# Feed-forward of odd chunks begun in the next batch's context attentions

## The reference, cut to what matters

```python
x = L0(x, ctx, ctx, fside, fside)      # 16 heads of 64 over 64 context rows, bias added twice, residual, LayerNorm
h1 = ln(x);  x = attn(h1, h1, ...) + x        # 16 heads of 32 over the 1024 rows; q, k, v and weights rounded to 8 bits
h2 = ln(x);  x = attn(h2, context, ...) + x   # the same over the 64 context rows
h3 = ln(x)
a, g = split(h3 @ ff_w1 + ff_b1)              # 512 -> 2 x 2048
x = a * gelu(g) @ ff_w2 + ff_b2 + x           # 2048 -> 512
```

## Time and profile before

| what | us |
|---|---|
| median of 3 runs | 3792.23 (3792.03 to 3795.36) |
| the profiled execution, its own time | 3793.03 |
| its span, first to last instruction | 3791.2 |
| context attention of chunk 2, chunk 3 | 116.4, 118.2 |
| self-attention and middle of chunk 2 | 164.0, 134.9 |
| self-attention and middle of chunk 3 | 168.2, 146.6 |
| context attention of chunk 4, chunk 5 | 114.8, 120.0 |
| self-attention and middle of chunk 4 | 162.5, 134.5 |
| context attention of chunk 6, chunk 7 | 115.1, 120.6 |
| self-attention and middle of chunk 6 | 164.1, 135.1 |

### The profile page before, as it was taken

The page is one execution under the profiler, slowest core; times in us unless marked ns, Lnnn a source line. Parts: engine busy times, 40 slices in busy tenths (PEclk is TensorE's granted clock), DMA queues, the critical chain, the costliest instruction groups (busy, mean ns, idle before and its releaser), DMA issues.

```text
span 3791.2 us, 50839 instructions
## 1 busy us (share of the span) xinstructions
PE 3003.7 (79%) x19712; PEld 2180.3 (58%) x19712; DVE 2182.8 (58%) x3575; ACT 1621.5 (43%) x2666; POOL 1328.7 (35%) x1025
## 2 busy tenths in 40 slices
PE   4446646779967799989967798989977798989999
PEld 4335433445756565755756565755756565755677
DVE  2334539778445568468455577468455577468431
ACT  3412126557422267357422267257322167257321
POOL 1132327445232234245231244245241244244221
PEclk8678765689988899989988899999988899999999
DMA  6883644312343332422343332432443322422334
GB/s 209 293 297 119 236 150 153 149 61 79 134 151 141 137 117 79 149 102 79 144 146 139 133 117 79 150 112 79 157 140 145 126 105 75 150 111 79 144 122 178
DMA packets 232046, 518.20 MB, mean 137 GB/s; under 512 B 96768, under 2 KB 117504, under 8 KB 209792
## 3 DMA queue, kind: packets, MB, share of 16 engines
q1 hardware_dynamic: 219392, 513.33, 37.2%
q10 hardware_dynamic: 12416, 1.62, 0.3%
HBM read 428.39 MB, written 82.31 MB: 135 GB/s over the span
## 4 chain that ended last, share of the span: by engine, by line
PE 58%; DVE 18%; issue 7%; ACT 6%; POOL 6%; DMA 4%; SPq 2%; ACTq 1%; POOLq 0%; DVEq 0%
PE psum L1494 16%; PE psum L1495 15%; PE psum L1496 15%; PE psum L1770 5%; DVE mx L1374 4%; PE psum L1760 3%; DVE w1T L1393 2%; PE psum L1784 2%; DVE stats L1263 1%; DVE den L1380 1%; DMA kept<-st_lo 1%; ACT e L1080 1%; DVE x L1259 1%; POOL rstd L767 1%; SPq L502 1%
## 5 line engine op out<-in xcount | busy, mean ns | idle before, releaser
L809 POOL TENSOR_SCALAR w1b<-e,rec 128x1024 f16<-128x1024 f32 x512 | 572.7, 1119 | 810.4 <-DVE rec L1382 699.3
L1374 DVE TENSOR_REDUCE mx<-psum 128x1 f32<-128x1024 f32 x512 | 624.6, 1221 | 216.9 <-PE psum L1761 214.4
L1080 ACT ACTIVATE e<-psum,nb,scale 128x1024 f32<-128x1024 f32 x512 | 616.7, 1205 | 16.7
L1494 PE MATMUL psum<-h_hi,fw_hi 128*128 128x512 f32 x1024 | 452.7, 442 | 2.2 <-DVE h_lo L1170 2.2
L1770 PE MATMUL psum<-ident,w1b 128*128 128x128 f16 x4096 | 348.1, 234 | 126.2 <-DVE w1T L1393 115.1
L1770 PEld LDWEIGHTS psum<-ident,w1b 128*128 128x128 f16 x4096 | 259.4, 104 | 270.2 <-issue 227.2
L1495 PE MATMUL psum<-h_lo,fw_hi 128*128 128x512 f32 x1024 | 411.2, 402 | 0.0
L1496 PE MATMUL psum<-h_hi,fw_lo 128*128 128x512 f32 x1024 | 411.0, 401 | 0.0
L1393 DVE TENSOR_SCALAR w1T<-psum 128x1024 bf16<-128x1024 f16 x512 | 347.1, 678 | 42.6 <-PE psum L1770 40.4
L1494 PE MATMUL psum<-w_hi,ht_hi 128*128 128x512 f32 x640 | 269.0, 420 | 71.0 <-DVE e L1317 37.2
L1259 DVE TENSOR_TENSOR x<-psum,x 128x512 f32<-128x512 f32 x224 | 152.7, 684 | 271.2 <-PE psum L1496 271.2
(11 more groups left out here) (170 smaller groups left out, 6070.8 us busy)
## 6 DMA issues: line engine op xcount, KB each, us to landing
fw_hi<-pieces SPq DMA_DIRECT2D x192, 512.0 KB, 3.2
fw_lo<-pieces SPq DMA_DIRECT2D x192, 512.0 KB, 4.2
w_hi<-kept SPq DMA_DIRECT2D x80, 1024.0 KB, 4.9
w_lo<-kept SPq DMA_DIRECT2D x80, 1024.0 KB, 7.6
fbias<-in_fside_Bx16xSxS SPq DMA_DIRECT2D x64, 256.0 KB, 3.8
prep_raw<-in_L_xattn_ff_w SPq DMA_DIRECT2D x12, 1024.0 KB, 8.0
pieces<-prep_hi SPq DMA_DIRECT2D x24, 512.0 KB, 3.5
pieces<-prep_lo SPq DMA_DIRECT2D x24, 512.0 KB, 5.5
```

What stands on the lines that cost most here:

```text
L809: pool.tensor_scalar(w1b[u % NH][:], e1[u % NE][:], rec1[:, u % 8:u % 8 + 1], HALF, ALU.mult, ALU.add).then_inc(w1_ready.sem, 1)
L1080: act.activation(e1[s % NE][:], psum[:, i:i + 2, :].rearrange("p i n -> p (i n)"), ACT.Exp, bias=nb1[:, s % 4:s % 4 + 1], scale=scale[:, 0:1],
L1374: dve.tensor_reduce(mx1[:, s % 4:s % 4 + 1], psum[:, i:i + 2, :].rearrange("p i n -> p (i n)"), AX, ALU.max).then_inc(maxed1.sem, 1)
L1494: pe.matmul(o, s_hi, m_hi, start=first, stop=False)
```

## The change

The feed-forward of chunks 1, 3 and 5 no longer waits for the self-attention of the next chunk. Its steps 0 to 7 are hosted by the first context attention of the next batch and 8 to 15 by the second; self-attention of chunk n + 1 hosts 18 steps (16 to 33), the middle 14. The plan `FROM_A` holds this. In each context attention one step stands behind the transposes of `x` and seven in the tail, 8, 7, 7 and 6 quarters ahead of the four `norm_T`. Chunks 0, 2, 4, 6 keep their 28 and 20 steps (`FROM_S`), chunk 7 is still alone.

Slot 2 of the blocks is in use in the context attentions, and with it buffers 0 and 1. A fourth buffer is laid over the queries and keys of the odd chunk, which are tensors of their own now (`q1_odd`, `k1_odd`). Pieces 0 to 7 of these three chunks go alternately through buffers 3 and 2; pieces 8 and later and the other chunks through 0 to 2, one place further on. Piece 0 is loaded in the middle of the odd chunk, once its self-attention is done; piece 1 in the last steps of that middle. VectorE waits for step 15 before it writes `q1_odd` again.

```diff
+LAG_T = 5
+A_SLOTS = 18
+A_TAIL = 12
...
+    for c in range(NC if in_A else 0):
+        for s in range(A_SLOTS):
+            ends.append(4 * in_A * c + (4 if s < A_TAIL else (12, 19, 26, 32)[min(s - A_TAIL, 3)]))
...
+FROM_S = host_quarters(0, 28, [s for s in range(M_SLOTS) if s not in (16, 21)])
+FROM_A = host_quarters(8, 18, (0, 1, 2, 3, 4, 6, 10, 11, 12, 13, 15, 16, 18, 20))
...
+def begins_in_A(n):
+    return n % NC == NC - 1 and n < CHUNKS - 1
...
+            if begins_in_A(n):
+                i = (3, 2)[v % 2] if v < 8 else (v - 8) % 3
+            else:
+                i = (v + 1) % 3
...
+        fourth = scope([("fw_hi3", [P, 1024], F32R), ("fw_lo3", [P, 1024], F32R)])
+        q1.append(sb("q1_odd", [P, HG, CH], BF16))
+        k1.append(sb("k1_odd", [P, HG, CH], BF16))
...
+                if r == F_RING:
+                    wait_filled(sp, ("a1", n, HG - 1))
...
+                else:
+                    for s in range(A_SLOTS):
+                        feed(NC * b - 1, FROM_A, A_SLOTS * c + s)
...
                 elif n > NC:
                     wait_filled(sp, ("q1", n, 3))
-                    for v in range(F_RING):
-                        load_piece(n - 2, v)
+                    for v in (8, 9):
+                        load_piece(NC * b - 1, v)
...
+                    if s == 2 and begins_in_A(n):
+                        load_piece(n, 0)
...
+                host(A_TAIL - 1)
                 dve.wait_ge(bias_added.sem, bias_added.at(("bo", n)))
                 for t in range(NT):
+                    host(A_TAIL + t)
                     residual_variance("o0", 0, n, t, EPS0)
...
+                if n % NC == NC - 1 and n > NC:
+                    wait_filled(dve, ("f", NC * (n // NC) - 1, PIECE_END[6]))
...
+                    host(1 + i)
                 for t in range(NT):
+                    host(A_TAIL + t)
                     norm_T("h1T", 1, n, t)
```

150 lines of the change are left out of this document (97 added, 53 removed).

## The result

| | before | after |
|---|---|---|
| median of the runs, us | 3793.74 | 3726.29 |
| lowest to highest | 3792.03 to 3795.36 (4 runs) | 3723.84 to 3738.10 (4 runs) |
| ratio, 95% interval | | 0.983, 0.9816 to 0.9841 |
| span of the profiled run | 3791.2 | 3722.5 |
| mean granted clock | 0.884 | 0.894 |

The change saves 67.5 us, against the 78.6 us forecast. The time lies 12 us above the 3714 us forecast and inside the range. The direction was right. Of the seven terms of the sum the one for self-attention was clearly too large, the one for the middle somewhat too small, and half of the one for the table loads measured nothing.

What follows compares the result with a forecast made beforehand. TensorE, busiest at 79% of the span, was taken to set self-attention's pace while idling in the context attentions. Seven terms gave -26.2 us a batch, three times -78.6: 3792.2 to 3714 us; own range 3690 to 3740, 8-in-10 range 3682 to 3768.

Steps and rivals of the forecast that it cites:

- the seven terms of the sum: Per batch: self-attention -21.4, middle -18.5, context attention's beginning -3.2, tails +5 and +7, tables +2.6, batch's edge +2.3 us.
- the one for self-attention: Self-attention of chunks 2, 4, 6: 64 units at 2.15 us plus 5 us for one gelu, 142.6 us, saving 21.4 us.
- the one for the middle: Middle of chunks 2, 4, 6: fewer hosted steps and a vanished wait save 18.5 of 134.9 us, bounds 10 and 22.
- the one for the table loads: Return to exponentials at the second context attention and at self-attention's start: 2 x 1.28 = +2.6 us a batch.

## What to carry to other kernels

Work that fills an engine's gaps also keeps its clock: before taking matmuls out of a stage, price its beginning and end apart from its steady part, and look for the count below which the stage grows longer again (here between 12 and 18 hosted steps). Where a step is hosted in a stage of short chains, walk each engine's queue in order; one gating ahead of a normalisation cost 4 us a batch. Look also for a small instruction with a long time: VectorE's `den` of 0.22 us took 3.2 us beside an addition on GpSimd. And try the longest wait that recurs first: the one for `x`, which only needed its transfer issued earlier, held 41 us, more than half of what the whole change brought.

## What the hardware showed that I had not expected

Fewer matmuls made the same stage longer: 18 hosted steps 149.0 us at a mean granted clock of 0.92, 12 hosted steps 156.0 us at 0.82, in all three batches (156.0, 156.7 and 151.4 us).

The same instructions took less time at a higher granted clock (first 11 units of the changed kernel: 25.2 us at 0.73, 23.8 us at 0.86), but a higher clock did not pay when it was bought with more matmuls: 16 units took 41.2 us at 1.00 and 37.9 us at 0.82 with fewer steps.

A VectorE instruction of 128x2 elements (0.22 us) took 2.54, 3.21 or 4.28 us while GpSimd added 128x2048 numbers to `x` (4.53 us), and ended 0.02 to 0.03 us after it each time. The maximum that VectorE took from PSUM beside the same addition kept its 1.23 us.

Issuing `x` earlier on SyncE took the whole wait away: behind the store and a 2 MB block TensorE waited 15 to 18 us at a batch's edge, ahead of them not at all.
